# A spectral block with attention: first part of the modes cut from 40 to 32 images, low modes' mixing moved to GpSimd

## The chip, the cores and the metric

One core of a Trainium2 chip. The metric is the device time of one execution in microseconds, lower is better. The engines are TensorE (PE; its weight loads are shown as PEld), VectorE (DVE), ScalarE (ACT), GpSimd (POOL) and SyncE (SP), which issues the DMAs. All arithmetic is float32. A matmul of float32 shows as two instructions in the trace.

## The reference

The input is x of shape 4 x 64 x 256 x 256. It is group-normalised over the last axis in 32 groups of 8 (statistics over the 64 images and the rows as well), and a block is added to it:

```python
xa_n = _inorm(xa)                                  # each of 256 images by itself
k, q = _spec_conv(xa_n, kw, (64, 64)), _spec_conv(xa_n, qw, (64, 64))
v = _spec_conv(xa_n, vw, (256, 256))               # rfft2, 16 x 8 low modes, irfft2
att = softmax(q k^T * 64) v                        # over the 64 images of a batch
att = _inorm(att) + xa
att_n = _inorm(att)
mix = _spec_conv(att_n, mix_w, (256, 256))         # 64 x 32 modes
skip = att_n * mix_skip_w
out = _inorm(_inorm(mix + skip)) + att
return x_normed_input + out
```

All normalisations after the first need only energies of modes (Parseval), so an image is transformed once, its 64 x 32 modes are weighed and summed, and one synthesis plus a scaled copy of x gives the output.

## The kernel before

Four batches b of 64 images are worked through. X holds the batch, one image of 256 x 256 as 128 partitions x 512 columns. A quad is four images; there are 16 quads u in a batch.

**The full part.** For a quad of batch b, in `produce`: `inverse_h` (L423) and `inverse_w` (L438) on PE make the synthesis, `keep_t` (L624) on ACT moves the half-way result T with a scale and a bias for the image; POOL's `scale_x` (L849) multiplies the image in X by its factor; DVE's `finish` (L1168) adds the two; SP stores it and loads the image of batch b+1 in its place. From quad LAG = 3 on, PE also does the `forward` transforms (L378) of batch b+1's quad u - 3, into the banks psY[0] and psY[1]; ACT squares those images (`square`, L600) and keeps the modes (`keep_y`, L593); DVE sums the squares (`sum_squares`, L939). On DVE the four sums of a quad stand before its four finishes. The last three quads' forward transforms stand behind quad 15. Batch 3 has no next batch, and DVE itself scales every fourth image from 16 on (`by_vector`), by factors that ACT makes (`vector_alphas`, L633).

Of the waits: `inverse_w(s)` waits until images up to 2s - 3 are finished; `finish` waits for POOL's scaling and PE's synthesis.

**The attention stage.** Between the last forward transform and the first synthesis stands `attend(b)`, on all engines at once: group statistics, low modes of q, k and v, logits (L522), maximum (L1057), Exp (L675), the probabilities' transpose (L527) and copy (L680), the attention product (L530), its squares (L686, L688), then on DVE a chain of scalars per image (64x1 instructions, L1067 to L1090, called the norm chain below), and the energies of the modes. For these the 64 images' modes are taken in eight groups g of 8: `raw_modes` (L399) and `turn_modes` (L410) on PE, `keep_raw` (L606) and `mode_powers` (L610) on ACT, `weigh_modes` (L949) on DVE, `weigh` (L830) and `add_products` (L835) on POOL, `turn_group` (L620) on ACT, `fold_powers` (L956) on DVE. The five instructions L1096 to L1100 mix the low modes on DVE (MA, d2).

**Two parts.** The factors of the images (SCL, BIA, C2) don't come for all 64 at once. With SPLIT = 5 the first part is 10 quads, 40 images, and needs groups 0 to 4: halve_energies, PE's `energy` (L453), `deviations` (L1126), ACT's `root` (L649), `coefficients` (L1131, which releases coef_made with a memset, L1142), PE's `spread` (L458), `keep_spread` (L1147), then POOL's `alphas` (L842) and the first scaling. `low_outputs` (L1144), `turn_low` (L463), `add_low` (L1157) and `low_piece` (L653) put the low modes into S in three PIECES: quad 0, quads 1 to 9, quads 10 to 15. For the second part the same steps are spread over quads: `second(b)` is 3, in batch 3 it is 1; deviations in that quad, root on ACT behind the squares of the next, coefficients two quads on (one in batch 3), spread, keep_spread and low_outputs three on, turn_low and add_low four on. POOL waits with image 24 for coef_made of the second part (L872).

**Order.** Each engine runs its instructions in the order written; semaphores alone bind them to each other. PE's second-part results lie in psY[1] (psY[0] in batch 3), so PE waits for y_kept before it writes there, and the next forward transform into that bank waits for var_made, c2_kept or d_added.

```python
                        if u == second(b) + 3:
                            spread(b, 1)
```

## Time and profile before

| what | us |
| --- | --- |
| median of three runs (lowest, highest) | 636.29 (633.12, 636.81) |
| the profiled execution | 633.88 |
| its span, first to last instruction | 632.1 |
| mean granted clock of TensorE | 0.961 of full |
| DVE / ACT / POOL busy | 482.8 / 356.6 / 336.4 |
| chain that ended last: PE / DVE / ACT / POOL / DMA | 53% / 25% / 7% / 5% / 5% |

The span is from the first to the last instruction on any engine; the time of an execution has about 1.8 us more. Busy shares are averages over stages that differ; a line can be a helper's, as L909 (tensor_tensor on DVE), L912 and L913 (tensor_scalar), L916 (scalar_tensor_tensor) and L919 (a dot product). A name out<-in is that of the tensor: the low-mode buffers A, MA and D, and RC, are slices of Y and show as Y; QKV, TMP and XL are slices of SQ.

### The profile page before, as it was taken

The page shows a single profiled execution, that of the slowest core. Times are in us where ns is not written, and L with a number is a line of the kernel's source. Part 1 is how long each engine was busy: PE and PEld are TensorE (multiplying, and loading weights), DVE is VectorE, ACT ScalarE, POOL GpSimd, SP SyncE. Part 2 cuts the span into 40 slices and gives each one's busy share as a digit, 9 for nine tenths or more (in the row PEclk, how much of TensorE's full clock was granted, in tenths as well). Part 3 has the DMA queues.
Part 4 walks back from the last instruction along what each step waited for, and adds up shares of the span by engine and source line. Part 5 has one row for each costly group of instructions (what it writes and reads, how often), then busy time and mean ns, then how long its engine had stood idle before and what let it go on. Part 6 is the DMA issues. An engine that isn't in the chain of part 4 may idle for free.

```text
span 632.1 us, 13832 instructions
## 1 busy us (share of the span) xinstructions
PE 581.8 (92%) x5072; PEld 480.6 (76%) x5072; DVE 482.8 (76%) x1095; ACT 356.6 (56%) x778; POOL 336.4 (53%) x398
## 2 busy tenths in 40 slices
PE   9999996999999996999999999699999999866994
PEld 9999644899899842789999874488999985354773
DVE  4666787787776888688777768777877768878996
ACT  6888353575666534466666635256576662543431
POOL 0270046959960014896975002597897200479993
PEclk9999996999999999899999999789999999979998
DMA  8993003899899901579999950279799993005787
GB/s 318 326 385 110 1 2 96 293 311 301 292 313 322 328 14 41 208 264 305 287 332 309 317 206 1 67 255 303 252 334 322 322 303 112 0 34 192 263 309 270
DMA packets 75522, 142.55 MB, mean 226 GB/s; under 512 B 6016, under 2 KB 6656, under 8 KB 75456
## 3 DMA queue, kind: packets, MB, share of 16 engines
q1 hardware_dynamic: 75456, 141.67, 65.6%
q8 instruction: 41, 0.67, 0.5%
q14 instruction: 25, 0.20, 0.1%
HBM read 74.54 MB, written 67.11 MB: 224 GB/s over the span
## 4 chain that ended last, share of the span: by engine, by line
PE 53%; DVE 25%; ACT 7%; POOL 5%; DMA 5%; issue 5%; SPq 0%; DVEq 0%; ACTq 0%; POOLq 0%
PE psY L386 23%; PE psP L448 15%; PE psT L433 7%; DVE QP L945 6%; DVE X L909 4%; ACT SQ L604 3%; POOL X L855 3%; DMA X<-in_x 3%; DVE Y L909 3%; DVE SQ L909 3%; DMA out<-X 2%; PE psP L494 1%; DVE IM L913 1%; DVE SQ L919 1%; DVE IM L916 1%
## 5 line engine op out<-in xcount | busy, mean ns | idle before, releaser
L855 POOL TENSOR_TENSOR X<-X,ALPHA 128x512 f32<-128x512 f32 x244 | 254.6, 1080 | 31.7 <-DVE IM L1142 18.5
L386 PE MATMUL psY<-FWD,X 128*128 128x128 f32 x1856 | 224.0, 279 | 2.3 <-DMA X<-in_x 2.2
L386 PEld LDWEIGHTS psY<-FWD,X 128*128 128x128 f32 x1856 | 213.1, 193 | 15.5 <-issue 13.9
L945 DVE TENSOR_REDUCE QP<-SQ 128x32 f32<-128x512 f32 x256 | 162.2, 680 | 48.3 <-ACT SQ L604 48.1
L909 DVE TENSOR_TENSOR X<-X,psP 128x512 f32<-128x512 f32 x192 | 125.8, 684 | 51.2 <-PE psP L448 23.9
L448 PE MATMUL psP<-INVW,T 64*128 64x256 f32 x768 | 141.9, 404 | 13.4 <-DVE X L909 7.8
L604 ACT ACTIVATE SQ<-X 128x512 f32<-128x512 f32 x232 | 132.4, 621 | 9.1 <-DVE Y L916 6.4
L833 POOL TENSOR_TENSOR Y<-Y,OMEGA 128x256 f32<-128x256 f32 x32 | 24.5, 765 | 189.0 <-ACT Y L612 189.0
L448 PEld LDWEIGHTS psP<-INVW,T 64*128 64x128 f32 x768 | 93.8, 191 | 34.2 <-ACT T L630 14.8
L630 ACT ACTIVATE T<-psT,BIA,SCL 128x256 f32<-128x256 f32 x128 | 65.3, 560 | 94.3 <-PE psT L433 89.8
L596 ACT ACTIVATE Y<-psY 128x512 f32<-128x512 f32 x128 | 76.2, 595 | 46.5 <-PE psY L386 45.3
L433 PE MATMUL psT<-INVH,Y 64*128 64x256 f32 x512 | 72.4, 402 | 0.0
L448 PE MATMUL psB<-INVW,T 64*128 64x256 f32 x256 | 68.9, 390 | 0.0
L433 PEld LDWEIGHTS psT<-INVH,Y 64*128 64x128 f32 x512 | 54.9, 203 | 5.2
L448 PEld LDWEIGHTS psB<-INVW,T 64*128 64x128 f32 x256 | 46.7, 190 | 0.0
L909 DVE TENSOR_TENSOR X<-X,psB 128x512 f32<-128x512 f32 x64 | 43.6, 682 | 1.8 <-POOL X L855 1.3
L838 POOL TENSOR_TENSOR Y<-Y 128x256 f32<-128x256 f32 x32 | 24.1, 754 | 19.7 <-DVE Y L909 19.4
L404 PE MATMUL psT<-Y,GWR 128*64 128x512 f32 x128 | 30.8, 600 | 0.0
L404 PE MATMUL psP<-Y,GWR 128*64 128x512 f32 x128 | 30.6, 598 | 0.0
L647 ACT ACTIVATE ALPHA<-ALPHA,ONES 128x256 f32<-128x256 f32 x32 | 16.2, 505 | 24.0 <-POOL ALPHA L846 24.0
L846 POOL TENSOR_TENSOR ALPHA<-MR,C 128x256 f32<-128x256 f32 x32 | 19.7, 616 | 15.0 <-DVE C L1155 11.3
L617 ACT ACTIVATE Y<-Y 128x128 f32<-128x128 f32 (+2 forms) x44 | 12.9, 293 | 23.4 <-POOL Y L838 16.6
(206 smaller groups left out, 552.5 us busy)
## 6 DMA issues: line engine op xcount, KB each, us to landing
X<-in_x SPq DMA_DIRECT2D x116, 512.0 KB, 5.4
out<-X SPq DMA_DIRECT2D x116, 512.0 KB, 3.9
X<-in_x SPq DMA_DIRECT2D x24, 256.0 KB, 4.2
Y<-in_x SPq DMA_DIRECT2D x6, 1024.0 KB, 5.1
out<-X SPq DMA_DIRECT2D x24, 256.0 KB, 3.8
INVH<-t_inv_h SPq DMA_DIRECT2D x1, 256.0 KB, 8.8
LW<-in_low_w SPq DMA_DIRECT2D x1, 204.0 KB, 5.7
FWD<-t_fwd SPq DMA_DIRECT2D x1, 128.0 KB, 2.1
```

Of the source, the lines that this page charges most:

```text
L386: last = mm(psY[p % 2][:, (2 * i + c) * 128:(2 * i + c + 1) * 128], image(nb, 2 * p + i)[:, a, c * 128:(c + 1) * 128], FWD[:, a, :], start ...
L404: last = mm(psR[m % 2][64 * t:64 * t + 64, :], GWR[:, c, k, :, :].rearrange("p r v -> p (r v)"), Y[:, c, k, 16 * m + 8 * t:16 * m + 8 * t ...
L433: last = mm(psT[h][:, 0:H], S[rows, q, part, :, :].rearrange("p j n -> p (j n)"), INVH[rows, part, :], start=part == 0, stop=part == 1)
L448: last = mm(out_bank(b, 2 * s + i)[:, W * a:W * (a + 1)], T[rows, s % 4, 128 * a:128 * (a + 1)], INVW[rows, :], start=True, stop=True)
L596: nc.scalar.activation(Y[:, :, :, i0:i0 + 3:2, :].rearrange("p c k i u -> p i (c k) u"), psY[p % 2][:, :].rearrange("p (i n u) -> p i n u" ...
L604: nc.scalar.activation(SQ[:, n % RING, :], flat_image(nb, n), ACT.Square).then_inc(squared, 1)
L630: nc.scalar.activation(T[:, p % 4, :], psT[p % 2][:, 0:H], ACT.Identity, bias=BIA[:, p:p + 1], scale=SCL[:, p:p + 1]).then_inc(t_kept, 1)
L833: P.tensor_tensor(v, v, over(OMEGA[:, 0:1], [[0, 4], [0, 2], [1, NV]]), MUL).then_inc(powers_weighted, 1)
L838: P.tensor_tensor(S[:, 2 * g:2 * g + 2, 0, :, :].rearrange("p q j n -> p q (j n)"), w[:, 0, :].rearrange("p (q n) -> p q n", q=2), w[:, 1, ...
L855: P.tensor_tensor(v, v, al, MUL).then_inc(x_scaled, 1)
L909: return V.tensor_tensor(out, a, b, op)
L945: V.tensor_reduce(QP[:, 4 * (k % 2) + place(n) % 4, :], SQ[:, n % RING, :].rearrange("p (a g j) -> p g a j", a=HC, j=GW), AX.XY, ADD).then ...
```

## The change

SPLIT goes from 5 to 4, so the first part is 32 images and the second 32; the pieces of the low modes become quad 0, 1 to 7, 8 to 15. One warming matmul goes. In the attention stage DVE takes the maximum and the probabilities first and does other work behind them; it copies the turned probabilities, and ACT copies two rows of INVW instead. ACT loads Exp's table early, by a one-column Exp. The attention is kept in ATT, a slice of QKV, and POOL's mix_low copies it to A and does the low mixing. PE's raw_modes, turn_modes, energy and inverse_h stand in another order. In the full part the second part's steps come in three successive quads.

The diff, cut to the lines that change and the functions they stand in, in the order PE, ACT, POOL, DVE; blocks inside spectral_block are indented less than in the file.

```diff
--- before.py
+++ after.py
...
-SPLIT = 5
-WARM = (2, 4)
+SPLIT = 4
+WARM = (2, 3)
...
+ATT = QKV[:, 2, :, :]
...
+low_mixed = sem("low_mixed")
...
 def factors(n):
-    return psY[1][:, GROUPS * q:GROUPS * q + 1] if q < 6 else psY[0][:, GROUPS * (q - 6):GROUPS * (q - 6) + 1]
+    return psY[1][:, GROUPS * q:GROUPS * q + 1] if q < 4 else psY[0][:, GROUPS * (q - 4):GROUPS * (q - 4) + 1]
...
     def energy(b, part):
-        pe.wait_ge(energy_part, 10 * b + (6, 10)[part])
+        pe.wait_ge(energy_part, 10 * b + (5, 10)[part])
...
+        if part:
+            pe.wait_ge(c2_kept, 2 * b + 2)
...
-        raw_modes(b, 1, (1, 2, 3))
+        raw_modes(b, 1, (1,))
...
-        turn_modes(b, 1)
...
-        raw_modes(b, 2, (0, 1, 2, 3))
+        raw_modes(b, 1, (2, 3))
+        raw_modes(b, 2, (0,))
+        turn_modes(b, 1)
+        raw_modes(b, 2, (1, 2, 3))
...
+        energy(b, 0)
...
-        raw_modes(b, 3, (1, 2, 3))
-        energy(b, 0)
+        raw_modes(b, 3, (1, 2))
...
+        raw_modes(b, 3, (3,))
+        inverse_h(b, 0)
...
-        inverse_h(b, 0)
...
     def produce(b, more):
-                if u == LAG + 4:
+                if u == LAG + 2:
...
-                if u == LAG + 5:
+                if u == LAG + 3:
...
-                if new and u in (LAG, LAG + 3, LAG + 4):
+                if new and u in (LAG, LAG + 2):
...
-                if u == second(b) + 3:
-                    spread(b, 1)
-                if u == second(b) + 4:
+                if u == second(b) + 2:
...
+                if u == second(b) + 1:
+                    if new:
+                        pe.wait_ge(y_kept, 32 * (b + 1) + 2 * (u - LAG) + 2)
+                    spread(b, 1)
...
-        for i in ((19, 23, 27, 31, 35, 39), (43, 47, 51, 55, 59, 63))[part]:
+        for i in ((19, 23, 27, 31), (35, 39, 43, 47, 51, 55, 59, 63))[part]:
...
+        nc.scalar.activation(IM[:, 21:22], IM[:, 20:21], ACT.Exp)
...
+        mode_powers(b, 1)
...
-        mode_powers(b, 1)
-        keep_raw(b, 1)
-        act.wait_ge(probs_turned, b + 1)
-        nc.scalar.activation(PR[:, 1, :], psB[0:IMGS, 320:384], ACT.Copy).then_inc(probs_kept, 1)
...
-        mode_powers(b, 2)
...
-        nc.scalar.activation(A.rearrange("p r n -> p (r n)"), psA[0:IMGS, 0:2 * LOW], ACT.Copy).then_inc(att_kept, 1)
-        turn_group(b, 0)
-        for m in range(2):
+        nc.scalar.activation(ATT.rearrange("p r n -> p (r n)"), psA[0:IMGS, 0:2 * LOW], ACT.Copy).then_inc(att_kept, 1)
+        def norm_root(m):
...
+        norm_root(0)
+        keep_raw(b, 1)
+        norm_root(1)
+        turn_group(b, 0)
+        mode_powers(b, 2)
+        mode_powers(b, 3)
+        turn_group(b, 1)
+        for k in range(2):
+            p = 64 * k + NV
+            nc.scalar.activation(INVW[p:p + 1, :].rearrange("p (g j) -> p g j", j=GW),
+                                 over(MR[p:p + 1, 1, 0:32], [[1, 32], [0, GW]]), ACT.Copy)
...
-        turn_group(b, 1)
-        for g in range(3, SPLIT):
-            mode_powers(b, g)
-            turn_group(b, g - 1)
-        turn_group(b, SPLIT - 1)
+        turn_group(b, 2)
...
-        mode_powers(b, SPLIT)
+        mode_powers(b, 4)
+        turn_group(b, 3)
+        mode_powers(b, 5)
...
-        mode_powers(b, SPLIT + 1)
...
-        turn_group(b, SPLIT)
+        turn_group(b, 4)
+        mode_powers(b, 6)
+        turn_group(b, 5)
...
     def produce(b, more):
-                mode_powers(b, SPLIT + 2)
+                mode_powers(b, 7)
...
-            if not more and u in (2, second(b) + 5):
+            if not more and u in (2, 6):
...
-                turn_group(b, SPLIT + 1 + u - second(b))
-            if u == second(b) + 4:
+                turn_group(b, 6 + u - second(b))
+            if u == LAG + 4:
...
-            if u == second(b) + 5:
+            if u == second(b) + 3:
...
-            if u == second(b) + 1:
+            if u == second(b):
...
+    def mix_low(b):
...
+        d2 = TMP[:, 1, :, :]
+        low_w = lambda r: over(LM[:, r, 0:1], [[0, 2], [1, LOW]])
+        pool.wait_ge(att_kept, b + 1)
+        pool.wait_ge(raw_made, 4 * b + 2)
+        P.tensor_tensor(MA, ATT, low_w(0), MUL).then_inc(low_mixed, 1)
+        P.tensor_tensor(d2, ATT[:, ::-1, :], low_w(1), MUL).then_inc(low_mixed, 1)
+        P.tensor_copy(A, ATT).then_inc(low_mixed, 1)
+        pool.wait_ge(low_mixed, 5 * b + 3)
+        for r, op in enumerate((SUB, ADD)):
+            P.tensor_tensor(MA[:, r, :], MA[:, r, :], d2[:, r, :], op).then_inc(low_mixed, 1)
...
     def batch(b):
-        for g in range(SPLIT + 1):
-            weigh(b, g)
-            if g == SPLIT:
-                alphas(b, 0)
-            add_products(b, g)
-        behind = {2: SPLIT + 1, 8 if b < B - 1 else 3: SPLIT + 2}
+        weigh(b, 0)
+        weigh(b, 1)
+        add_products(b, 0)
+        add_products(b, 1)
+        mix_low(b)
+        weigh(b, 2)
+        weigh(b, 3)
+        add_products(b, 2)
+        add_products(b, 3)
+        weigh(b, 4)
+        alphas(b, 0)
+        add_products(b, 4)
+        weigh(b, 5)
+        add_products(b, 5)
+        behind = {2: 6, 8 if b < B - 1 else 4: 7}
...
-        do(ts(XL2, XL.rearrange("p r n -> p (r n)"), 2.0, None, MUL))
-        do(tt(XO, XL, over(OLOW[:, 0:1], [[0, 2], [1, LOW]]), MUL))
-        wait_link()
-        do(ts(XL2[:, ::LV], XL2[:, ::LV], 0.5, None, MUL))
-        do(dot(DUMP, XO, XL, 1.0, im(26)))
-        for k in range(2):
-            p = 64 * k + NV
-            row = INVW[p:p + 1, :].rearrange("p (g j) -> p g j", j=GW)
-            do(V.tensor_copy(row, over(MR[p:p + 1, 1, 0:32], [[1, 32], [0, GW]])))
...
-        weigh_modes(b, 0)
...
-        fold_powers(b, 0)
+        do(ts(XL2, XL.rearrange("p r n -> p (r n)"), 2.0, None, MUL))
...
+        do(tt(XO, XL, over(OLOW[:, 0:1], [[0, 2], [1, LOW]]), MUL))
+        dve.wait_ge(probs_turned, b + 1)
+        V.tensor_copy(PR[:, 1, :], psB[0:IMGS, 320:384]).then_inc(probs_kept, 1)
+        wait_link()
+        do(ts(XL2[:, ::LV], XL2[:, ::LV], 0.5, None, MUL))
+        weigh_modes(b, 0)
...
-        fold_powers(b, 1)
+        do(dot(DUMP, XO, XL, 1.0, im(26)))
...
-        do(dot(DUMP, A, low3(XL2, 2), 2.0, im(15)))
-        weigh_modes(b, 2)
+        wait_link()
+        do(dot(DUMP, ATT, low3(XL2, 2), 2.0, im(15)))
...
-        do(dot(DUMP, A, XO, 2.0, im(27)))
-        do(dot(TMP[:, 1, :, :], QKV[:, 0, :, :], over(OLOW[:, 0:1], [[0, 2], [1, LOW]]), 1.0, im(30)))
+        do(dot(DUMP, ATT, XO, 2.0, im(27)))
+        do(dot(QKV[:, 1, :, :], QKV[:, 0, :, :], over(OLOW[:, 0:1], [[0, 2], [1, LOW]]), 1.0, im(30)))
...
-        fold_powers(b, 2)
...
-        weigh_modes(b, 3)
-        d2 = TMP[:, 1, :, :]
-        low_w = lambda r: over(LM[:, r, 0:1], [[0, 2], [1, LOW]])
-        do(tt(MA, A, low_w(0), MUL))
-        do(tt(d2, A[:, ::-1, :], low_w(1), MUL))
-        wait_link()
-        for r, op in enumerate((SUB, ADD)):
-            do(tt(MA[:, r, :], MA[:, r, :], d2[:, r, :], op))
-        fold_powers(b, 3)
-        for g in range(4, SPLIT):
-            weigh_modes(b, g)
+        weigh_modes(b, 2)
+        for g in range(SPLIT):
...
+        weigh_modes(b, 3)
...
-        low_outputs(b)
+        low_outputs(b, 0)
+        weigh_modes(b, 4)
...
-        weigh_modes(b, SPLIT)
+        weigh_modes(b, 5)
...
-        fold_powers(b, SPLIT)
-        weigh_modes(b, SPLIT + 1)
-        fold_powers(b, SPLIT + 1)
...
+        fold_powers(b, 4)
+        fold_powers(b, 5)
...
     def halve_energies(b, part):
-        dve.wait_ge(energy_part, 10 * b + (5, 9)[part])
+        dve.wait_ge(energy_part, 10 * b + (4, 9)[part])
...
-    def low_outputs(b):
+    def low_outputs(b, part):
+        if part == 0:
+            dve.wait_ge(low_mixed, 5 * b + 5)
...
     def keep_spread(b, part):
-        dve.wait_ge(products, 8 * b + q1 // 2)
+        dve.wait_ge(turned, 8 * b + q1 // 2)
...
-            dve.wait_ge(vector_alpha, 1 + (n >= 40))
+            dve.wait_ge(vector_alpha, 1 + (n >= 32))
...
     def produce(b, more):
-                weigh_modes(b, SPLIT + 2)
+                weigh_modes(b, 6)
+                fold_powers(b, 6)
+            if u == 1:
+                weigh_modes(b, 7)
...
-                fold_powers(b, SPLIT + 2)
+                fold_powers(b, 7)
...
-                    if n % 4 == (2 if more else 1):
-                        second_part(b, u, more)
+                    second_part(b, u, n % 4, 2 if more else 1)
...
-    def second_part(b, u, more):
-        if u == second(b):
+    def second_part(b, u, i, late):
+        if (u, i) == (second(b), late):
...
-        if u == second(b) + (2 if more else 1):
+        if (u, i) == (second(b) + 1, 0):
...
-        if u == second(b) + 3:
+            low_outputs(b, 1)
+        if (u, i) == (second(b) + 1, 3):
...
-            low_outputs(b)
-        if u == second(b) + 4:
+        if (u, i) == (second(b) + 2, late):
```

## Rows read from the trace of the kernel before

**Rows 1.** Page, part 1: busy us, share, instructions of PE.

```profile
PE 581.8 (92%) x5072; PEld 480.6 (76%) x5072; DVE 482.8 (76%) x1095; ACT 356.6 (56%) x778; POOL 336.4 (53%) x398
```

**Rows 2.** Windows, two stages: us, five engines' busy us, PEclk, DMA share, GB/s.

```profile
66.00:107.40 41.40, 34.04 (x280) 19.19 (x279) 32.69 (x122) 16.40 (x48) 13.38 (x18) 0.89 0.08 27
...
131.60:205.30 73.70, 73.70 (x696) 67.62 (x696) 55.98 (x100) 48.77 (x95) 46.01 (x46) 1.00 0.93 307
```

**Rows 3.** Timeline, first attention: start us, us, engine, line, operation, idle before.

```profile
80.76 0.82 PE L522 MATMUL psB<-Y 72*64 72x64 f32 x8
...
83.32 0.21 DVE L1057 TENSOR_REDUCE IM<-psB 64x1 f32<-64x64 f32 x1
...
86.19 0.67 PE L530 MATMUL psT<-SQ,T 64*64 64x272 f32 x2
...
87.58 0.18 DVE L916 SCALAR_TENSOR_TENSOR IM<-IM 64x1 f32<-64x1 f32 x1 [1.92 <-ACT SQ L688]
```

**Rows 4.** Timeline, DVE, first attention, from the last normalisation to the energy.

```profile
92.51 0.40 DVE L959 TENSOR_REDUCE FP<-Y 128x4 f32<-128x256 f32 x1
...
92.83 0.67 DVE L909 TENSOR_TENSOR Y<-psY,MIX 128x512 f32<-128x512 f32 x1
...
93.43 0.42 DVE L909 TENSOR_TENSOR Y<-Y,LM 64x272 f32<-64x272 f32 x1
...
93.78 0.96 DVE L909 TENSOR_TENSOR SQ<-Y,LM 64x272 f32<-64x272 f32 x1
...
97.05 0.45 DVE L909 TENSOR_TENSOR Y<-FP,ROWS 128x64 f32<-128x64 f32 x1
```

**Rows 5.** Timeline, POOL and DVE, where both work, first attention.

```profile
88.99 0.73 POOL L838 TENSOR_TENSOR Y<-Y 128x256 f32<-128x256 f32 x1 [1.24 <-DVE Y L909]
...
89.25 0.72 DVE L916 SCALAR_TENSOR_TENSOR IM<-IM 64x1 f32<-64x1 f32 x2
...
91.03 0.46 DVE L916 SCALAR_TENSOR_TENSOR IM<-IM 64x1 f32<-64x1 f32 x2
```

**Rows 6.** Tile LM: POOL line, operation, count, ns min/median/max, start, form.

```profile
L803 POOL TENSOR_TENSOR T<-LM x1: 407/407/407, 34.4 to 34.4; 64x136 f32<-64x136 f32 x1
```

**Rows 7.** Timeline, POOL, first scalings of batch 0.

```profile
104.31 2.10 POOL L855 TENSOR_TENSOR X<-X,ALPHA 128x512 f32<-128x512 f32 x2
...
107.74 6.24 POOL L855 TENSOR_TENSOR X<-X,ALPHA 128x512 f32<-128x512 f32 x6
```

**Rows 8.** Timeline, PE: spread and first forward transforms (batches 0, 1).

```profile
100.59 0.74 PE L460 MATMUL psT<-Y,SIDE 64*128 64x96 f32 x2 [2.76 <-DVE IM L1142]
...
117.94 3.84 PE L386 MATMUL psY<-FWD,Y 128*128 128x128 f32 x32
...
268.30 3.84 PE L386 MATMUL psY<-FWD,Y 128*128 128x128 f32 x32
...
277.53 2.05 PE L386 MATMUL psY<-FWD,Y 128*128 128x128 f32 x16 [0.21 <-DVE IM L913]
```

**Rows 9.** Timeline, ACT, DVE, PE, around quad 4 of batch 0.

```profile
129.28 0.19 ACT L651 ACTIVATE IM<-IM 64x1 f32<-64x1 f32 x1
...
130.03 1.28 DVE L909 TENSOR_TENSOR X<-X,psP 128x512 f32<-128x512 f32 x2 [0.57 <-PE psP L448]
...
131.59 3.84 PE L386 MATMUL psY<-FWD,X 128*128 128x128 f32 x32
```

**Rows 10.** Timeline, DVE coefficients twice (batches 0, 3), PE, DVE (batch 3).

```profile
140.04 0.37 DVE L912 TENSOR_SCALAR Y<-PAIR,IM 64x32 f32<-64x32 f32 x2
...
577.07 1.84 DVE L912 TENSOR_SCALAR Y<-PAIR,IM 64x32 f32<-64x32 f32 x2
...
581.50 0.45 PE L448 MATMUL psP<-INVW,T 64*128 64x256 f32 x1 [3.45 <-DVE X L909]
...
593.90 1.28 DVE L909 TENSOR_TENSOR X<-X,psP 128x512 f32<-128x512 f32 x2
```

**Rows 11.** Windows, batch 3 behind PE's longest idle time: columns as rows 2.

```profile
583.00:586.00 3.00, 3.00 (x16) 2.84 (x15) 2.28 (x4) 0.00 (x0) 3.00 (x4) 0.50 1.02 379
```

## Prediction

> **What bounds the kernel now.** I read the page's engine part, the windows by stage, the chain of waits, and then the timeline of each engine in the stages where the diff works. TensorE (PE) is busy 581.8 of 632.1 us [rows 1], but the windows split this. Between 131.6 and 205.3 us PE has no idle time at all and DMA is at 0.93: every quad of four images takes 6.7 us, whatever the others do. In the attention stage, 66 to 107.4 us, PE has 7 us idle and GpSimd (POOL) 28, and the granted clock averages 0.89 [rows 2]. There the chain goes through VectorE (DVE). So a batch is a DVE chain of about 40 us, a ramp in which DVE and POOL feed PE, and a part in which any PE wait is lost. The fourth batch has no forward transforms; its last ten quads are a DVE and PE loop. The end is shifted by three things: how early the ramp starts, what PE waits inside the full part, and when the last batch's loop starts. The profiled execution took 633.88 us around a span of 632.1; the sum below is made against 633.9.
>
> **Attention, what leaves the path.** Times are batch 0's; the others repeat them. The logits end at 81.58 but DVE takes them at 83.32, behind the doubling of XL, a dot product, two INVW copies and weigh_modes(0) [rows 3]. After the change the maximum is taken at once, Exp's table is already loaded, the probabilities' copy comes from DVE, and turn_modes(1) is no longer ahead of the attention product: it ends at about 84.3 instead of 86.86 [rows 3], 2.6 us sooner. DVE then still owes weigh_modes(0), (1) and the dot product moved behind it, and starts the norm at 85.45 instead of 87.58 [rows 3]: 2.1 gained. weigh_modes(2) goes out of the norm chain, 0.6 (the step from 92.83 to 93.43). Behind the norm, from 92.51 to 97.05, stood a fold of 0.32, two more, two weighings of 0.6, and the low mixing: 0.35, 0.9, and two additions of 0.46 [rows 4]. Of these 4.54 us the new code has one weighing and four folds, 0.6 + 4 x 0.33 = 1.9, so 2.6 is gained; weigh_modes(3) between halving and deviations costs 0.3, the shorter halving gives 0.2 back. Sum: 2.1 + 0.6 + 2.6 - 0.3 + 0.2 = 5.2 us, if nobody gets in DVE's way.
>
> **Attention, what is added.** mix_low puts five instructions on POOL, which had been idle, just while DVE goes through the norm. Price on POOL: 64x136 took 0.41 us [rows 6] and 128x256 took 0.73 [rows 5], so two of 272 columns at 0.73, a copy of 272 at about 0.5 (0.4 to 0.8), two of 136 at 0.41: 2.8, with the self-wait 2.9. It starts when the attention is kept and raw_modes(1) is done, near 86.2. POOL's work by itself is in time: weigh(2) and (3) would end near 90.7, and the fold that needs the latter comes at 91.2, 0.5 us later; above 3.4 us for mix_low this cover is gone, and each further microsecond is one on the path.
> The larger cost is that the two engines meet. DVE's scalar_tensor_tensor at 89.25, two inputs in SBUF, issued during a POOL addition that ran from 88.99 to 89.72; two took 0.72 us where two with POOL idle took 0.46 [rows 5], so the first ended only with POOL's instruction. The 64x272 product at 93.78 took 0.96 against 0.42 for the same form just before [rows 4], again under a POOL instruction. In the new order eight such DVE instructions (five scalar_tensor_tensor, three dot products) stand in the norm chain, beside add_products(1), the five of mix_low and two weighings on POOL: eight against eight. Laid side by side by hand, each DVE instruction waits for the end of the POOL instruction under way, 3.6 us in all. The lower end is 0 (they slip between); if each arrives at random, half an instruction of 0.6 us on average, 8 x 0.3 = 2.4. The nearest row has the full wait, the phase is unsure, so I take 3.0.
> The Trainium skill, "SBUF — State Buffer", section "SBUF: two separate sides", states that a DVE instruction with two SBUF inputs and a GpSimd instruction that reads SBUF exclude each other for their whole length. By that rule the term would be the full 3.6, and my sum 2.4 us longer over the four batches; rows 5 agree with it for one place.
> So the first part's coefficients come 5.2 - 3.0 = 2.2 us sooner (spread at 98.4, was 100.59 [rows 8]).
>
> **From the coefficients to the ramp.** POOL now does weigh(5) and add_products(5) behind alphas(0), where before weigh(5) lay under the coefficients, and weigh_modes(4) stands ahead of keep_spread: 0.7 + 0.5 = 1.2 us later to the first scaling, which thus starts 1.0 us sooner than 104.31. weigh(6) then waits about 0.1 for PE's turn_modes(3), now behind inverse_h(0). Image 2, 107.74 before [rows 7], starts at about 106.9, 0.8 sooner. From there POOL's 1.04 us an image [rows 7] sets when DVE finishes and PE may write the next bank: image 7 is finished 6.9 us later, inverse_w(5) takes 1.1, and PE starts batch 1's forward transforms at 115.0 instead of 117.94 [rows 8]. That is 3.0 us, more than POOL's 0.8, since in batches 0 and 2 PE lost time at half clock here, which I expect gone: its idle time before the energy is one stretch and not two. Batch 1, where POOL set the pace before, started at 268.30; 0.8 + 0.6 = 1.4 us sooner. add_low's wait for turned instead of products, the larger third piece (16 instead of 12 images) and four fewer columns in turn_low cost and give under 0.1 each. products(5), which releases the load ahead, and energy_part(8) come no later than now, 10 us before PE needs them: nothing.
>
> **Inside the full part (batches 0 to 2).** Here the closer steps cost. Before, the second coefficients were two quads behind the deviations, and spread one quad behind them. Now:
> First, PE waits for var_made in the quad after the first, whose finish on DVE follows POOL's image 14: 0.95 us, where batch 1 waited 0.2 to 0.4 [rows 8] and batches 0 and 2 nothing.
> Second, coefficients come right after finish(16), and PE's spread right after inverse_w(9). PE has 1.7 us of work between giving DVE image 16 and wanting spread; DVE needs 0.6 for the finish and 1.65 for the coefficients. That alone is 0.65 with the hand-over. But root(1) on ACT moves from after quad 4's squares (129.28) to before keep_t(8) [rows 9]; it waits for var_made, and behind it queue keep_t, add_one, turn_group, four squares and keep_y, for which DVE's sums wait, which stand before finish(16). In the trace those sums ended 0.57 ahead of finish(16) at 130.03 [rows 9]; with ACT held 3 to 4 us they end 2.2 behind where PE would have let it go. And POOL is still scaling images 16 to 23: two coefficient instructions took 0.37 us in batch 0 with POOL waiting, 1.84 in batch 3 with POOL running [rows 10]; only the last part of this falls under POOL here, 0.6. Sum 0.65 + 2.2 + 0.6 = 3.45 us of PE wait. Ends: 0.65 and, if all four coefficient instructions meet POOL, 5.7.
> Third, the psY[1] transforms of quad 5 wait for c2_kept, behind low_outputs and three finishes: 0.5.
> The energy, spread and turn_low matmuls are the same work in other quads. PE works from 131.59 on without a gap [rows 9], so nothing of the 4.9 us (4.5 in batch 1) comes back. Balance: batch 0: 3.0 - 4.9 = -1.9; batch 1: 1.4 - 4.5 = -3.1; batch 2 as batch 0: -1.9.
>
> **Batch 3.** second is one quad, POOL starts 1 us sooner, and the coefficients come after finish(8) instead of (9), no longer behind ACT's vector_alphas. They still run under POOL, 4.5 us. DVE reaches the even loop (593.90 [rows 10]) 0.9 us sooner: 3.9 without the 3.0 of waits. Ends 0 and 4.
>
> **Sum.** -1.9 - 3.1 - 1.9 + 0.9 = -6.0: slower, 633.9 + 6.0 = 639.9 us. The median of three runs, 636.3, lies 2.4 above the profiled one and their range is 3.7, so I give 641.
>
> **Rivals.**
> A: the engines don't meet. DVE's instructions slip between POOL's and the attention is 5.2 us shorter. For it: in rows 5 only the first of two waited. Against: both rows. Then 4 x 3.0 comes back: 641 - 12 = 629. This is the one on the other side, faster. It decides at the norm chain: below 1.5 us of waits (half) the whole is no slower than before.
> B: the wait for spread is short (0.65), since POOL's pace rather than ACT's squares orders DVE. 3 x 2.8 back: 641 - 8.4 = 632.6. Against: the queue behind root(1) is in order.
> C: PE's clock falls. In batch 3 an idle stretch of 3.45 us [rows 10] was followed by 3 us at a granted 0.50, which is 1.2 of 2.4 GHz [rows 11]. Now each attention has such a stretch before the energy and each full part one before spread, seven places; 3 us at half clock are 1.5 of work, some of it under DVE: 7 x 1.3 = 9. 641 + 9 = 650.
>
> **Chances.** Forecast 0.40, A 0.18, B 0.17, C 0.20, the rest 0.05. Faster by over 1% (below 630, about what can be told from no change): half of A and a little of B, 0.18. Slower by over 1% (above 642.7): C and 0.4 of the forecast's, 0.36. Within: 0.46. Range: 628 to 651, the likeliest case's own 636 to 646.
>
> **What would show it.** In the changed profile: the attention product ends 2.6 us after the logits' maximum is free to start; scalar_tensor_tensor of 64x1 longer than 0.3 us beside POOL's LM lines; spread near 98.4; first forward near 115; in quad 4 a PE idle row of 3 to 4 us released by DVE's memset, and ACT's root before keep_t. If spread is near 95.5, A holds; if PE's idle row is under 1 us, B; if PEclk shows 0.5 after the two idle stretches, C. A total below 630 would make the forecast wrong.

## The result: slower, above the forecast's range

The changed kernel takes 658.89 us (median of six executions, 650.55 to 660.37) against 635.48 for the kernel before on the same chip: a ratio of 1.0327, 95% interval 1.0282 to 1.0371. The ratio is taken over all executions but the slowest of the six, so it isn't that of the two medians, 1.037. The forecast was 641, with a range of 628 to 651. The profiled execution happens to be the shortest of the six, 650.55 us around a span of 648.5, so its trace shows 16.4 us of the loss (648.5 - 632.1), and a second trace, taken later (under "The changed kernel a second time"), shows the rest.

The page's first part and its row of the granted clock, the changed kernel (against [rows 1]):

```profile
PE 583.8 (90%) x5064; PEld 477.8 (74%) x5064; DVE 483.2 (75%) x1075; ACT 358.2 (55%) x786; POOL 346.4 (53%) x418
...
PEclk9999999979999998998999999999999999987999
```

PE has 2 us more of busy time and 14 us more without work. Where that lies is read from PE's timeline: the forward transforms mark the ends of each stage. Of the kernel before, the last ones ahead of the first two attentions (the first ones behind are in [rows 8]):

```profile
62.09 3.82 PE L386 MATMUL psY<-FWD,X 128*128 128x128 f32 x32
...
214.11 3.82 PE L386 MATMUL psY<-FWD,X 128*128 128x128 f32 x32
```

PE's timeline of the changed kernel, batch 0 and the start of batch 1:

```profile
62.46 3.82 PE L388 MATMUL psY<-FWD,X 128*128 128x128 f32 x32
...
94.78 0.28 PE L457 MATMUL psT<-ONES,Y 128*64 128x1 f32 x2 [2.79 <-DVE Y L945]
...
96.08 3.49 PE L406 MATMUL psP<-Y,GWR 128*64 128x512 f32 x8
...
116.73 3.84 PE L388 MATMUL psY<-FWD,Y 128*128 128x128 f32 x32
...
126.36 2.05 PE L388 MATMUL psY<-FWD,Y 128*128 128x128 f32 x16 [0.62 <-DVE IM L949]
...
134.83 0.71 PE L462 MATMUL psY<-Y,SIDE 64*128 64x96 f32 x2 [3.51 <-DVE IM L1162]
135.84 6.13 PE L388 MATMUL psY<-FWD,X 128*128 128x128 f32 x32
...
146.22 3.84 PE L388 MATMUL psY<-FWD,X 128*128 128x128 f32 x32
...
220.91 3.82 PE L388 MATMUL psY<-FWD,X 128*128 128x128 f32 x32
...
275.06 3.84 PE L388 MATMUL psY<-FWD,Y 128*128 128x128 f32 x32
```

From the end of the last forward transform to the start of the next batch's first one is the attention stage with its ramp; from there to the end of the next last one is the full part. The first attention took 117.94 - 65.91 = 52.03 us before and 116.73 - 66.28 = 50.45 now; the first full part 217.93 - 117.94 = 99.99 before and 224.73 - 116.73 = 108.00 now. All stages, worked out in this way from the traces (us; "again" is the second trace of the changed kernel, "filled" and "spaced" are two of the experiments, "best" the fastest version):

| stage | before | changed | again | filled | spaced | best |
| --- | --- | --- | --- | --- | --- | --- |
| attention 0, 1, 2 | 52.0, 50.4, 51.9 | 50.5, 50.3, 49.1 | 50.5, 51.6, 52.7 | 49.2, 50.0, 49.1 | 50.5, 51.3, 51.7 | 48.4, 47.5, 47.4 |
| full part 0, 1, 2 | 100.0, 101.6, 100.8 | 108.0, 107.7, 106.6 | 108.7, 108.4, 107.4 | 105.1, 105.5, 105.3 | 101.9, 101.2, 102.1 | 101.0, 102.3, 101.4 |
| last stage | 109.5 | 110.0 | 111.3 | 110.4 | 113.3 | 108.6 |

The full parts lost 8.0 + 6.1 + 5.8 = 19.9 us and the attentions gave 1.6 + 0.0 + 2.8 = 4.4 back. In quad 4 the two waits are in the lines above, 0.62 us for the deviations and 3.51 for the spread, the same to 0.02 us in all three batches: 3 x 4.13 = 12.4 of the 20 us. And behind the second wait a pair of transforms that takes 3.84 us at full clock takes 6.13. What the clock did there, from the windows of the changed kernel (columns as [rows 2]; the third number from the end is the granted clock):

```profile
96.00:100.00 4.00, 4.00 (x16) 1.19 (x12) 3.17 (x12) 1.05 (x4) 0.86 (x2) 0.57 0.01 2
133.00:141.00 8.00, 6.17 (x29) 6.08 (x30) 5.72 (x17) 1.57 (x4) 4.64 (x6) 0.57 0.56 160
...
294.00:298.00 4.00, 4.00 (x23) 4.00 (x23) 2.93 (x9) 0.96 (x2) 2.08 (x3) 0.57 0.77 202
451.00:455.00 4.00, 4.00 (x23) 4.00 (x23) 2.95 (x9) 1.39 (x3) 2.31 (x3) 0.57 0.77 231
```

The same of the kernel before, in two attentions and in its first full part:

```profile
98.00:112.00 14.00, 10.68 (x114) 8.77 (x116) 8.69 (x28) 5.34 (x17) 10.27 (x13) 0.51 0.45 148
...
402.00:416.00 14.00, 10.81 (x116) 8.90 (x118) 8.60 (x27) 5.47 (x17) 10.39 (x13) 0.51 0.49 150
```

```profile
131.60:139.00 7.40, 7.40 (x66) 6.83 (x65) 5.60 (x9) 5.01 (x11) 2.46 (x3) 1.00 0.91 307
```

A granted clock of 0.57 over a stretch is mostly the lower level, 1.2 GHz. In the kernel before PE ran some 27 us at it in the attentions of batches 0 and 2, and 7 in that of batch 1, a stage in which the chain goes through DVE and POOL for much of the time, and not at all in the full part. In the changed kernel the falls have moved: one behind the energy's wait in the attention (8 instructions of raw_modes took 3.49 us there, and spread could only follow at 99.50, 1.2 us after the coefficients were there), and one behind the spread's wait in each full part, where PE is the bound and every half-speed microsecond costs half of itself. Half clock took (1 - 0.57) x 4 = 1.7 us there in each of batches 1 and 2. In batch 0 it is (1 - 0.57) x 8 = 3.4, but the clock had fallen 1.0 us before the wait ended at 134.83, so 0.5 of it fell on a PE that had nothing to do, and 2.9 were lost: 6.3 of the 20 us in all.

The meeting of DVE and POOL in the norm chain, timeline of the changed kernel, DVE and then POOL:

```profile
85.55 0.66 DVE L952 SCALAR_TENSOR_TENSOR IM<-IM 64x1 f32<-64x1 f32 x1
...
87.16 0.99 DVE L952 SCALAR_TENSOR_TENSOR IM<-IM 64x1 f32<-64x1 f32 x2
...
89.47 1.93 DVE L952 SCALAR_TENSOR_TENSOR IM<-IM 64x1 f32<-64x1 f32 x2
...
86.56 0.85 POOL L862 TENSOR_TENSOR Y<-SQ,LM 64x272 f32<-64x272 f32 x1 [0.37 <-PE psP L406]
87.38 0.75 POOL L863 TENSOR_TENSOR SQ<-SQ,LM 64x272 f32<-64x272 f32 x1
...
88.57 1.19 POOL L867 TENSOR_TENSOR Y<-Y,SQ 64x136 f32<-64x136 f32 x2
```

Two such DVE instructions take 0.46 us when POOL rests [rows 5]; here 0.99 and 1.93.

And ACT's root ahead of keep_t in quad 4 of the changed kernel, with the sums on DVE that wait for the squares behind it, the finish of image 16 behind the sums, and PE's matmuls for image 16, which that finish also needs:

```profile
126.34 0.20 ACT L660 ACTIVATE IM<-IM 64x1 f32<-64x1 f32 x1 [5.14 <-DVE IM L949]
...
128.87 1.28 DVE L981 TENSOR_REDUCE QP<-SQ 128x32 f32<-128x512 f32 x2 [1.97 <-ACT SQ L613]
...
131.52 0.68 DVE L945 TENSOR_TENSOR X<-X,psP 128x512 f32<-128x512 f32 x1
...
128.46 1.13 PE L450 MATMUL psP<-INVW,T 64*128 64x256 f32 x8
```

PE's matmuls for image 16 in the kernel before, where DVE's finish began at 130.03 [rows 9]:

```profile
128.79 1.14 PE L448 MATMUL psP<-INVW,T 64*128 64x256 f32 x8
```

So PE had image 16 ready at 129.59 in the changed kernel and DVE took it 1.93 us later; in the kernel before it was 0.10 us later. DVE's sums held it up by 1.83.

### The profile page after: what moved, and what is told of

Same layout as the page of the kernel before. It is cut to its first block and busy times, and to the rows that moved or that the text cites. A ratio compares the mean times of both kernels' runs of the same rounds, so it can differ in the third digit from the quotient of the medians.

```text
span 648.5 us, 13834 instructions
## 1 busy us (share of the span) xinstructions
PE 583.8 (90%) x5064; PEld 477.8 (74%) x5064; DVE 483.2 (75%) x1075; ACT 358.2 (55%) x786; POOL 346.4 (53%) x418
## 5 line engine op out<-in xcount | busy, mean ns | idle before, releaser
L388 PE MATMUL psY<-FWD,X 128*128 128x128 f32 x1856 | 228.6, 282 | 4.2 <-DMA X<-in_x 3.2
L388 PEld LDWEIGHTS psY<-FWD,X 128*128 128x128 f32 x1856 | 217.6, 196 | 16.7 <-issue 11.6
L435 PE MATMUL psT<-INVH,Y 64*128 64x256 f32 x512 | 68.5, 385 | 5.3 <-ACT Y L627 5.3
L435 PEld LDWEIGHTS psT<-INVH,Y 64*128 64x128 f32 x512 | 52.2, 191 | 13.2 <-ACT Y L627 8.8
L873 POOL TENSOR_TENSOR ALPHA<-MR,C 128x256 f32<-128x256 f32 x32 | 19.7, 614 | 49.2 <-ACT ALPHA L656 25.6
L406 PE MATMUL psP<-Y,GWR 128*64 128x512 f32 x128 | 35.4, 656 | 0.0
L945 DVE TENSOR_TENSOR Y<-psY,MIX 128x512 f32<-128x512 f32 x24 | 16.0, 681 | 14.4 <-ACT Y L621 14.4
L388 PE MATMUL psY<-FWD,Y 128*128 128x128 f32 x192 | 23.8, 280 | 1.9 <-DVE IM L949 1.9
```

The source lines that it names most:

```text
L388: last = mm(psY[p % 2][:, (2 * i + c) * 128:(2 * i + c + 1) * 128], image(nb, 2 * p + i)[:, a, c * 128:(c + 1) * 128], FWD[:, a, :], start ...
L406: last = mm(psR[m % 2][64 * t:64 * t + 64, :], GWR[:, c, k, :, :].rearrange("p r v -> p (r v)"), Y[:, c, k, 16 * m + 8 * t:16 * m + 8 * t ...
L435: last = mm(psT[h][:, 0:H], S[rows, q, part, :, :].rearrange("p j n -> p (j n)"), INVH[rows, part, :], start=part == 0, stop=part == 1)
L945: return V.tensor_tensor(out, a, b, op)
```

## The experiments

Ratios are against the kernel before, run on the same chip; differences between versions below are taken between these ratios, at 634 us.

| version | median us | ratio (95%) |
| --- | --- | --- |
| changed | 658.89 | 1.0327 (1.0282 to 1.0371) |
| changed, root later | 653.85 | 1.0281 (1.0211 to 1.0352) |
| changed, steps spaced | 635.94 | 1.0039 (1.0008 to 1.0071) |
| changed, both idle stretches filled | 642.97 | 1.0142 (1.0097 to 1.0186) |
| changed, mixing later | 649.10 | 1.0240 (1.0200 to 1.0280) |
| changed, POOL held | 648.39 | 1.0245 (1.0199 to 1.0291) |
| changed, POOL held and root later | 642.98 | 1.0160 (1.0132 to 1.0187) |
| changed, only the full part's stretch filled | 649.31 | 1.0240 (1.0196 to 1.0283) |
| before, steps close | 651.58 | 1.0282 (1.0220 to 1.0343) |
| before, attention filled | 630.98 | 0.9960 (0.9936 to 0.9984) |
| spaced, mixing later, filled (best) | 623.70 | 0.9844 (0.9811 to 0.9877) |
| best without the fills | 626.71 | 0.9898 (0.9857 to 0.9938) |
| best with the change's mixing | 630.45 | 0.9942 (0.9918 to 0.9966) |

### Steps spaced again

```diff
-                        if u == second(b) + 2:
+                        if new and u == second(b) + 2:
+                            spread(b, 1)
+                        if u == second(b) + 2 + int(new):
                             turn_low(b, 1)
                         inverse_w(b, 2 * u + 1)
...
-                if (u, i) == (second(b) + 1, 0):
+                if (u, i) == (second(b) + 1, 2 if more else 0):
                     coefficients(b, 1)
                     low_outputs(b, 1)
```

> The changed kernel with its 32-image first part and its attention stage kept, but in batches 0 to 2 the second part's steps further apart again: root behind the squares of quad 4, coefficients after finish(18), spread in quad 5 (before inverse_w(11)), turn_low in quad 6, and POOL's factors of group 4 asked for at image 28 instead of 24. Theory (the closer steps cost 4.1 us of PE waits and 1.6 to 3.2 us of half clock in each full part): both go, 3 x 6.4 = 19 us sooner than the changed kernel's profiled 650.5, so 631 to 636, no slower than the kernel before. Rival (the smaller first part is what costs: POOL runs out of work or waits for factors it had before): POOL's wait for group 4 or DVE's for images 32 on shows in the full part, and the time stays above 643.

635.94 us, ratio 1.0039: 18 us below the changed kernel, and 0.4% above the kernel before. The waits for the spread are gone in batches 0 to 2 and the full parts are back at 101.2 to 102.1 us. The theory stands. The full parts are 2.8 us longer in all than the kernel before's, so the smaller first part costs little there. The last stage was 3.8 us longer in this execution, the second longest of ten; it was not taken apart.

### The kernel before with close steps

```diff
+            def close_part(b, u, i):
+                if (u, i) == (LAG, 2):
+                    deviations(b, 1)
+                if (u, i) == (LAG + 1, 0):
+                    coefficients(b, 1)
+                    low_outputs(b)
+                if (u, i) == (LAG + 1, 3):
+                    keep_spread(b, 1)
+                if (u, i) == (LAG + 2, 2):
+                    add_low(b, 2)
```

(with spread at the end of quad 4, turn_low in quad 5 and the root ahead of quad 4, as in the change)

> The kernel before with one part of the change alone: in batches 0 to 2 the second part's steps in three successive quads, as the change has them (40 images in the first part, attention stage and batch 3 untouched). Theory (this part alone makes the loss): PE waits 0.6 us for the deviations and 3.4 for the spread, the clock falls behind it, and each full part takes 106 to 108 us instead of 100 to 101.6: 633.7 + 3 x 6.5 = 653, between 648 and 656. Rival (it needs the 32-image first part to hurt): below 643.

651.58 us, ratio 1.0282, full parts of 106.9, 105.9 and 105.1 us, 15.6 us more than the kernel before's. PE's timeline of this kernel, quad 4 of batch 0, and a window behind the wait:

```profile
136.49 0.43 PE L460 MATMUL psY<-Y,SIDE 64*128 64x96 f32 x2 [3.50 <-DVE IM L1145]
...
137.10 5.38 PE L386 MATMUL psY<-FWD,X 128*128 128x128 f32 x32
```

```profile
137.00:141.00 4.00, 4.00 (x23) 3.90 (x22) 3.48 (x9) 0.28 (x1) 4.00 (x5) 0.58 0.63 180
```

The wait of 3.50 and the lower clock behind it are the ones of the changed kernel. One part of the change alone makes 2.8 of the 3.3%, and taking that part out of the change gives 2.9 back.

### Filling PE's idle stretches

```diff
+            def keep_busy(bank, n):
+                for _ in range(n):
+                    mm(bank[:, 0:128], ONES[:, :], ONES[:, :], start=True, stop=True)
...
+                pe.wait_ge(att_kept, b + 1)
+                keep_busy(coef_bank(b, 0), 10)
                 energy(b, 0)
...
                                 pe.wait_ge(y_kept, 32 * (b + 1) + 2 * (u - LAG) + 2)
+                                keep_busy(coef_bank(b, 1), 13)
                             spread(b, 1)
```

> The changed kernel with matmuls nobody reads put into PE's two idle stretches: 10 of 128 columns (2.4 us) ahead of the energy in each attention stage, 13 (3.1 us) ahead of the second spread in batches 0 to 2. No wait is shortened. Theory (the granted clock falls after these stretches, 1.2 us in batch 0's attention and 3.2, 1.6, 1.6 us in the full parts, and in other executions more, which gives the two groups of times near 651 and 659): half clock is gone behind them, mean granted clock 0.985 or more, time 642 to 646 and the two groups become one. Rival (the idle time alone costs, the clock falls where DVE has the path anyway): time stays at 650 to 659.

642.97 us. The window behind the spread's wait, which showed 0.57 above, in the filled kernel:

```profile
133.00:141.00 8.00, 7.67 (x94) 6.74 (x94) 6.96 (x18) 2.73 (x6) 4.64 (x6) 1.00 0.70 215
```

No result waits less, and yet 1.0327 - 1.0142 = 1.85%, 12 us, are back. The full parts still take 105.1 to 105.5 us: these are the waits themselves. They are 6.4 us shorter in all than the changed kernel's, as much as half clock had taken there by the windows, 6.3. One of the four executions took 647.18 us at a mean clock as high as the others', so not all of the spread between executions is the clock. In the attention the spread came at 98.44, and the first forward transform started at 115.59.

With the 13 in the full part alone (the attention's ten left out):

> The changed kernel with the 13 matmuls nobody reads ahead of the second spread only, nothing in the attention stage (the run with both gave 643.0). Theory (most of the half clock is behind the spread's wait, in a part where PE never idles): 644 to 648, and the rest of the way to 643 belongs to the attention. Rival (the clock falls behind the attention's stretch as much, and what is kept in one place is lost in the other): 650 or more.

649.31 us, above the 644 to 648 expected. By the ratios the full part's fill gives 0.87% and the attention's another 0.98%. Either figure is known to 0.6% at best, so the two can't be told apart. The theory, that most of the half clock's cost is behind the spread's wait, isn't borne out: near the median the clock falls for longer in the attentions than in the first trace (below).

The kernel before, filled in the same way (8 ahead of the energy, 9 ahead of the first part's spread):

> The kernel before with 8 and 9 matmuls nobody reads ahead of the energy and of the spread of each attention stage (its idle stretches of 2.4 and 2.8 us). Theory (the kernel before paid for half clock too, in its attentions, where batches 0 and 2 took 52.0 and 51.9 us against 50.4 in batch 1): batches 0 and 2 come to 50.4, about 3 us sooner in all, 0.5%. Rival (it didn't): same time.

630.98 us, 0.4% less than the kernel before, 2.5 us. The window that was at 0.51 is now at full clock:

```profile
98.00:112.00 14.00, 11.93 (x158) 10.15 (x158) 10.89 (x31) 6.59 (x19) 10.81 (x13) 1.00 0.48 137
```

Its three attentions took 49.5 us each, 5.8 us less in all, of which the full parts (102.0, 102.0, 102.7) took 4.3 back; why they did was not tried. In those attentions the kernel before had 34 us at half clock, in which PE can do 17 us of work less, and filling shortened them by 5.8, a third; at the end of the kernel 2.5 us of it arrived. In the changed kernel's full parts 6.3 were lost and 6.4 came back. The time at half clock says little; where it lies says more. And with both kernels filled the attentions are nearly as long without the change (49.5 us) as with it (49.2, 50.0, 49.1): most of what batches 0 and 2 gained in the filled changed kernel was the clock, and the rest some 0.4 us each.

### The spread's wait: ACT's root and POOL's scaling

The root moved back behind the squares of the next quad:

```diff
-                    if u == second(b):
+                    if u == second(b) + int(more):
                         root(b, 1)
```

> The changed kernel, with ACT's root of the second part moved back behind the squares of the next quad (batches 0 to 2). Theory (ACT queued behind the root holds the squares, and they hold DVE's sums ahead of finish(16)): PE's wait for the second spread falls from 3.5 us to 1.3 in each of three batches, 3 x 2.2 = 6.6 us sooner or a little more where the clock no longer falls, so a ratio to the kernel before of 1.022 instead of 1.033. Rival (POOL's scaling paces finish(16), the squares were late by nobody's fault): the wait stays within 0.5 us of 3.5 and the time within 2 us of the changed kernel.

653.85 us, 1.0281 where 1.022 was expected: the rival was right on the wait. (By the ratios the time is 2.9 us below the changed kernel's, which lies within their intervals.) Timeline of this kernel, quad 4, POOL, DVE, PE:

```profile
124.75 8.32 POOL L882 TENSOR_TENSOR X<-X,ALPHA 128x512 f32<-128x512 f32 x8
...
130.10 0.94 DVE L949 TENSOR_SCALAR Y<-PAIR,IM 64x32 f32<-64x32 f32 x1
...
131.27 1.83 DVE L948 TENSOR_SCALAR Y<-PAIR,IM 64x32 f32<-64x32 f32 x2
...
133.53 0.43 PE L462 MATMUL psY<-Y,SIDE 64*128 64x96 f32 x2 [3.37 <-DVE IM L1162]
```

The sums on DVE did wait 1.35 us less, 0.62 instead of 1.97. But the coefficients then ran in the midst of POOL's scaling. POOL ends an image at 124.75 + 1.04 k, so at 131.0, 132.0 and 133.1; the three matrix instructions of the coefficients ended at 131.04 and, the last two, at 133.10: each waited for the end of the image under way. In the changed kernel the coefficients came so late that POOL stopped (at image 24, 134.2 us) under the third of them. The wait fell by 0.14 us.

POOL held back instead (its wait for the coefficients moved from image 24 to 20):

```diff
-                        if i == 4 * LAG + 12 and b < B - 1:
+                        if i == 4 * LAG + 8 and b < B - 1:
                             pool.wait_ge(coef_made, 2 * b + 2)
```

> The changed kernel with POOL's wait for the second coefficients moved from image 24 to image 20, so that it scales nothing while DVE makes them. Theory (each DVE coefficient instruction on a matrix ends only with POOL's scaling of an image; the root's place and POOL's scaling stand behind each other, which is why moving the root alone gave 0.14 us): the coefficients take 1.8 instead of 2.6 us and PE's wait for the spread becomes 2.7 to 2.8 us. Rival (POOL is needed: images 20 to 23 come late): DVE waits for image 20 in quad 5 and PE loses there what it gained.

PE's timeline of this kernel, quad 4 of batch 0:

```profile
133.79 0.71 PE L462 MATMUL psY<-Y,SIDE 64*128 64x96 f32 x2 [2.59 <-DVE IM L1162]
```

648.39 us. The wait is 2.59 us in all three batches, 0.9 less. Half clock still followed each of them in the profiled execution (651.62 us, the longest of the four), for 6.8 us in batches 0 and 2 and 3.4 in batch 1, and its full parts took 108.0, 105.1 and 107.8 us. So the median's gain is not the wait's alone. Both edits together:

> Both: POOL waits for the second coefficients at image 20, and ACT's root stands behind the squares of the next quad. Theory (ACT's queue 1.4 us and POOL's scaling 2.0 us each hide the other): coefficients in 1.8 instead of 3.8 us, PE's wait for the spread falls from 3.4 to about 1.4 us in three batches, some 6 us in all and the clock falls less, 641 to 648 in all. Rival (PE's wait is set by the three steps following each other alone): it stays above 2.5 us.

Timeline of this kernel, quad 4, POOL, DVE, PE:

```profile
124.35 4.18 POOL L882 TENSOR_TENSOR X<-X,ALPHA 128x512 f32<-128x512 f32 x4
130.94 4.38 POOL L882 TENSOR_TENSOR X<-X,ALPHA 128x512 f32<-128x512 f32 x4 [2.40 <-DVE IM L1162]
...
128.61 0.68 DVE L945 TENSOR_TENSOR X<-X,psP 128x512 f32<-128x512 f32 x1
...
129.70 0.28 DVE L949 TENSOR_SCALAR Y<-PAIR,IM 64x32 f32<-64x32 f32 x1
...
130.21 0.37 DVE L948 TENSOR_SCALAR Y<-PAIR,IM 64x32 f32<-64x32 f32 x2
...
126.90 1.14 PE L450 MATMUL psP<-INVW,T 64*128 64x256 f32 x8
...
131.00 0.43 PE L462 MATMUL psY<-Y,SIDE 64*128 64x96 f32 x2 [1.24 <-DVE IM L1162]
```

The coefficients' three matrix instructions take 0.65 us, where they took 2.77 with the root moved alone and 1.58 in the changed kernel, and PE waits 1.24. The two causes hide each other: root alone -0.14, POOL alone -0.92, both -2.27 us. Not all of the 1.24 is the steps' closeness: PE has image 16 ready at 128.04 and DVE takes it at 128.61, 0.57 later where the kernel before needs 0.1, since its sums still wait 0.62 and 0.17 us for ACT's squares. So 0.47 is still the sums, and 0.77 is left for the closeness, worked out from these rows. No half clock followed the waits of 1.24 us. The full parts fell to 102.8 to 103.9 us and the whole to 642.98 us, 1.0160. The rivals (POOL is needed; the steps alone set 2.5) fell.

The Trainium skill, "SBUF — State Buffer", section "Who interferes with whom", names tensor_scalar among the DVE instructions that can take the ports that GpSimd needs, and says that whoever comes second waits for the other's whole instruction. The rows above agree for the 64x32 instructions; the 64x1 instructions between them, 0.20 to 0.27 us in both kernels, did not wait.

### The mixing on POOL

```diff
-                mix_low(b)
                 weigh(b, 2)
                 weigh(b, 3)
                 add_products(b, 2)
                 add_products(b, 3)
+                mix_low(b)
```

> The changed kernel with POOL's five low-mixing instructions moved behind add_products(3), past the norm chain. Theory (DVE's instructions with two inputs in SBUF wait for POOL's): the norm chain on DVE, 6.9 us from 85.5 to 92.4, shortens by 1.5 to 2.3 us, since POOL has only two additions and two weighings left beside it; the spread of the first part comes as much sooner if PE's clock doesn't fall, 4 x 1.5 to 2 us = 6 to 8 sooner. Rival (POOL's other additions and weighings, now sooner, meet DVE just the same): under 0.5 us a batch, and the mixing then delays coefficients or the first scaling.

649.10 us. DVE's norm chain went from 85.04 to 92.42 in the changed kernel, 7.4 us, and from 86.41 to 92.02 here, 5.6: 1.8 less, as expected. Of four times that 0.87%, 5.5 us, arrived; PE then waited 1.0 us for the mixed low modes, which were now late.

The same question at full clock, asked of the best version below, with the mixing put back:

> The fastest version so far (spaced steps, filled stretches, 623.7) with POOL's mixing put back where the change has it, beside DVE's norm chain, and 10 instead of 4 filling matmuls ahead of the energy, whose wait is the longer for it, so that the clock stays. Theory (the meeting of DVE and POOL costs 1.8 us of norm chain a batch, which reaches the end): 4 x 1.8 = 7 us, 629 to 632. Rival (POOL's later work hides it): under 3 us, below 627.

630.45 us, 0.98% or 6.2 us more than 623.70 (with six more filling matmuls under the longer wait for the energy). The two pairs of scalar_tensor_tensor, with the change's mixing, and in the best version:

```profile
87.66 1.00 DVE L965 SCALAR_TENSOR_TENSOR IM<-IM 64x1 f32<-64x1 f32 x2
...
89.98 1.92 DVE L965 SCALAR_TENSOR_TENSOR IM<-IM 64x1 f32<-64x1 f32 x2
```

```profile
88.17 0.46 DVE L964 SCALAR_TENSOR_TENSOR IM<-IM 64x1 f32<-64x1 f32 x2
...
89.68 0.95 DVE L964 SCALAR_TENSOR_TENSOR IM<-IM 64x1 f32<-64x1 f32 x2
```

### The changed kernel a second time

The changed kernel itself, twice:

> The changed kernel itself, looked at again. Its six executions lay in two groups, 650.6 and 652.0, and 658.5 to 660.4, with mean granted clocks of 0.972 and 0.958; only one of the first group has a profile. Theory (the same idle stretches, in more of them the clock falls, or for longer): in a profile near 659 the waits of PE are the same to 0.3 us each, and the 8 us are matmuls at half clock in the full parts and the attention stages. Rival (another wait is longer in these executions, a transfer's or POOL's): a wait of PE in the full part is longer by microseconds, at the same clock.

> As the run above, a second look at the changed kernel: with four of six executions in the slower group, two looks should meet it at least once. The same is expected of it.

659.26 and 656.90 us. Of PE's list of waits, first the profiled execution of above, then the one of 659.26 us:

```profile
PE psY L462 <- DVE IM L1162: 12.4, 4, 3.5
...
PE psY L388 <- DMA X<-in_x: 3.2, 4, 1.4
```

```profile
PE psY L462 <- DVE IM L1162: 12.5, 4, 3.5
...
PE psY L388 <- DMA X<-in_x: 5.7, 5, 1.8
```

And a window of its third attention, which in the shorter execution had full clock from 408 to 416 us:

```profile
414.00:421.00 7.00, 6.54 (x29) 3.46 (x30) 4.71 (x17) 1.37 (x6) 1.45 (x2) 0.51 0.00 0
```

The waits for the spread and for the energy are the same to 0.1 us in all. Of the 9.0 us between the two spans 5.0 lie in the attentions, where the clock fell in more of the same places, 2.2 in the full parts, 1.3 in the last stage and 0.5 ahead of the first attention; PE waited 2.5 us more for loads. So both held in part: mostly the clock, some of it transfers. Why those took longer was not tried.

### A version that beats both

Spaced steps; POOL's mixing between add_products(2) and (3); filling matmuls in the attention (4 ahead of the energy, 5 ahead of inverse_h(0)) and in batch 3:

```diff
                 add_products(b, 2)
+                mix_low(b)
                 add_products(b, 3)
...
+                keep_busy(psT[0], 256, 5)
                 inverse_h(b, 0)
...
                         if not new and u == second(b) + 1:
+                            keep_busy(coef_bank(b, 1), 0, 9)
                             spread(b, 1)
```

> The attempt at a version that beats both: the changed kernel with the second part's steps spaced as in the run above that had them apart, POOL's mixing between add_products(2) and (3) and so behind the norm chain, and matmuls nobody reads in PE's idle stretches of the attention stage (4 ahead of the energy, 5 ahead of inverse_h(0)) and of batch 3 (4, 9 and 9 ahead of the energy, of inverse_w(4) and of the spread). Theory: the spaced kernel's 636 less 4 x 1.5 of norm chain and 3 to 5 of half clock in batch 3 and in the attentions: 626 to 630, faster than before by 1%. Rival (POOL's scaling or the forward transforms' loads set the start of the full part): within 3 us of the spaced kernel.

623.70 us, 1.6% faster than the kernel before, and more than was expected. The attentions took 47.4 to 48.4 us. Without the fills:

> The fastest version so far without its filling matmuls: spaced steps and POOL's mixing behind the norm chain alone. Theory (the fills only keep the clock, worth 3 to 6 us; the mixing's place 4 to 6 of the spaced kernel's 635.9): 628 to 632. Rival (the fills gave nearly all of the 12 us between the spaced and the fastest version): 633 or more.

626.71 us, 1.0% faster than before with no work added. Against the spaced kernel the mixing's place alone gives 1.4%, 8.9 us, more than the 7.2 of norm chain: PE's wait for the energy fell from 2.8 to 1.0 us, and in the first three attentions the clock fell once, where it had fallen in each.

## Why the prediction was wrong, and where it was right

**The step that failed** is the clock's place in the sum. The balance had "in batches 0 and 2 PE lost time at half clock here, which I expect gone", and the fall behind the new idle stretches was rival C, at 0.20, as if the waits could come without it. It is no alternative to the waits but their consequence: a term that adds to them. With it the forecast was 650 (640 + 9, and one for the median), which is what the shortest executions show, though partly by luck: they have 2 us less of waits in the full parts than the forecast, and more half clock. C's own size was too small as well: 7 x 1.3 = 9 us, where filling two kinds of stretch gave 12 us and left the clock falling in batch 3. Against the kernel before, the forecast had -7.4 us for the attentions, +14.3 for the full parts and -0.9 for the last stage; the first trace shows -4.4, +19.9 and +0.5, the second, near the median, +0.5, +22.1 and +1.8. That a fall costs most in the full part, where PE never waits, was in my own rows (no idle time from 131.6 on [rows 2]) and not used.

**The waits in the full part** were right in size: 0.95, 3.45 and 0.5 forecast, 0.62, 3.51 and none measured, 4.1 against 4.9 a batch. The split of the 3.45 was near, too: closeness 0.65 forecast and 0.77 measured, DVE's sums behind ACT's squares 2.2 and 1.83, POOL 0.6 and 0.92, by the rows above. What it had wrong is what an edit of one of them is worth. The root's place holds 1.35 of the 1.83, but with the root moved alone the coefficients come under POOL's scaling and lose nearly all of it there: the root's place alone gives 0.14, POOL alone 0.92, both 2.27.

**The attention** was near where the clock let it be: the filled kernel's took 2.8, 0.3 and 2.8 us less than before, against 3.0, 1.4 and 3.0. The spread was forecast at 98.4 and came at 98.44 in the filled kernel; the forward transforms at 115.0, and came at 115.59 there, whose first attention began 0.5 us later than that of the kernel before. The meeting of DVE and POOL, forecast at 3.0, is 2.7 in the norm chain by the durations (0.66 instead of 0.23 us for one scalar_tensor_tensor, 0.99 and 1.93 instead of 0.46 each for the pairs, 0.70 instead of 0.43 for a dot product), and 0.6 more between the energy and the spread (a 64x64 instruction took 0.57 instead of 0.24 us, a 64x32 one 0.80 instead of 0.56), which I had not counted. In batch 1 the clock of the filled kernel still fell once, at 256.6 us. In the changed kernel as it is the three attentions gave 4.4 us instead of 7.4, and in the longer execution they took 0.5 us more than before.

**Batch 3** was to give 0.9 and took 0.5 in the one execution, 1.8 in the other, with half clock behind its waits.

**The rivals.** The 0.18 for "half of A and a little of B" was added up wrongly: half of A is 0.09. A (the engines don't meet) fell: they meet, for 1.8 us that moving the mixing takes away. B (the spread's wait is short) fell: 3.5 us in every batch. C happened, and on top of the forecast.

## What to carry to other kernels

When steps of a dependent chain are moved closer together, count the wait and then what the bounding engine does behind it: on TensorE an idle stretch may be paid a second time at half clock, and most where it had no idle time before. Two engines that block a third in turn must be taken away together; an edit that gives nothing alone is no proof that its cause was none. Where GpSimd and VectorE hold each other up as here, work moved to GpSimd belongs behind a chain of small VectorE instructions on the path, not beside it.

## What the runs showed of the hardware that I had not expected

The same kernel, with the same waits of PE for the energy and the spread to 0.1 us, had its clock fall behind the energy's wait of 2.8 us in some batches and executions and not in others: full clock from 408 to 416 us in one, 0.51 from 414 to 421 in the other. So a single profile of such a kernel can be 8 us from its median.

A DVE tensor_scalar of 64x32, one tensor and per-row scalars, waits for GpSimd's tensor_tensor on other data to end, 0.94 instead of 0.28 us, while those of 64x1 beside it don't.

Matmuls whose result nobody reads, in stretches where PE waits anyway, made one kernel 1.85% faster.
